# Attention on Trainium2: one Exp over four PSUM banks in place of two over two banks each

## The reference, cut to what matters

```
# per sequence: x is (2048, 1024), 16 heads of 64
h    = layernorm(x)
q    = h @ Wq + bq
k    = (h @ Wk + bk) @ Wl + bl
v    = (h @ Wv + bv) @ Wl + bl
attn = softmax(q k^T / 8)                # per head, 2048 x 2048
x    = x + layernorm((attn v) @ Wo + bo)
h2   = layernorm(x)
ffn  = h2 @ base_W.T + base_b
     + (h2 @ shared_A.T) @ shared_B.T
     + sum over the top 2 of 6 experts: weight * (h2 @ A_e.T) @ B_e.T
out  = x + layernorm(ffn)
```

## Time and profile before

| | |
|---|---|
| time of the runs, median (lowest to highest) | 4710.9 us (4707.45 to 4715.0) |
| the profiled execution's own time | 4704.67 us |
| its span, first to last instruction, core 7 (slowest) | 4703.1 us |
| spans of the other cores | 4646.7 to 4702.5 us |
| PE busy | 2743.8 us (58%) |
| DVE busy | 1551.9 us (33%) |
| ACT busy | 1297.1 us (28%) |
| stage B0, from its first QK to the last output projection's end | about 483 to 1865 us |
| stage B1, likewise | about 2322 to 3677 us |
| Exp: instructions, mean | 1024, 1.20 us |

### The profile page before, as it was taken

How to read it: one execution, slowest core, us unless ns; L and a number is a source line. 1 busy time by engine, 2 the same in 40 slices (tenths; PEclk the granted TensorE clock), 3 DMA queues, 4 the chain that set the end, 5 groups by cost and what they waited for, 6 DMA issues and landing times.

```text
span 4703.1 us, 32867 instructions; the slowest of 8 cores (4646.7 to 4703.1 us)
## 1 busy us (share of the span) xinstructions
PE 2743.8 (58%) x9296; PEld 843.8 (18%) x9296; DVE 1551.9 (33%) x2164; ACT 1297.1 (28%) x1117; POOL 10.1 (0%) x16
## 2 busy tenths in 40 slices
PE   4777566666666665667766566656666233333333
PEld 1333111111111111233211111111111111111111
DVE  2444122123222222444222322222222355444455
ACT  0000443443443443000144344454344000000000
POOL 0000000000000000000000000000000000000000
PEclk9888555555555555888955655665655666666666
DMA  5000100000000001100100000000000421222221
GB/s 108 19 18 2 17 0 0 18 0 0 18 0 18 0 0 32 40 19 19 18 0 0 18 0 0 18 0 0 18 0 0 112 88 73 80 81 90 90 76 67
DMA packets 52838, 137.00 MB, mean 29 GB/s; under 512 B 7479, under 2 KB 7614, under 8 KB 52670
## 3 DMA queue, kind: packets, MB, share of 16 engines
q1 hardware_dynamic: 42206, 117.59, 6.8%
q0 software_dynamic: 10464, 17.32, 2.3%
HBM read 101.87 MB, written 50.33 MB: 32 GB/s over the span
## 4 chain that ended last, share of the span: by engine, by line
PE 47%; DVE 23%; ACT 13%; issue 7%; ACTq 5%; DMA 4%; DVEq 1%; SPq 0%; another core or an unknown queue 0%; POOL 0%; POOLq 0%
PE ps L323 12%; ACT pt_sb L438 12%; DVE xn_fm L477 9%; PE ps L457 6%; PE ps L421 6%; PE ps L460 5%; PE psT L421 5%; ACTq L165 4%; PE ps L517 3%; PE ps L862 3%; PE ps L483 3%; DVE xn_fm L475 2%; DMA xst<-z_scr 1%; DVE k_sb L590 1%; DVE k_sb L894 1%
## 5 line engine op out<-in xcount | busy, mean ns | idle before, releaser
L438 ACT ACTIVATE pt_sb<-ps,cst_sb 128x1024 bf16<-128x1024 f32 x512 | 616.6, 1204 | 1311.8 <-PE ps L425 1279.5
L475 DVE COPY xn_fm<-ps 1x1024 f32<-1x1024 f32 x64 | 78.0, 1219 | 1845.5 <-PE ps L460 1845.5
L438 ACT ACTIVATE pt_sb<-psT,cst_sb 128x1024 bf16<-128x1024 f32 x512 | 616.0, 1203 | 136.9 <-PE psT L425 136.6
L457 PE MATMUL ps<-pt_sb,vt_sb 128*65 128x512 bf16 x1024 | 625.3, 611 | 40.2 <-ACTq L165 40.2
L460 PE MATMUL ps<-pt_sb,vt_sb 128*65 128x512 bf16 x1024 | 621.7, 607 | 0.0
L421 PE MATMUL ps<-q_sb,k_sb 64*128 64x512 bf16 x512 | 288.8, 564 | 411.9 <-ACTq L165 371.5
L483 PE MATMUL ps<-xn_fm,ones_sb 1*64 1x512 f32 x128 | 123.8, 1069 | 519.6 <-DVEq L165 519.6
L477 DVE RECIPROCAL xn_fm<-xn_fm 1x1024 f32<-1x1024 f32 x64 | 418.6, 6541 | 5.1
L323 PE MATMUL ps<-xn_fm,arena 128*128 128x512 bf16 x1536 | 354.4, 394 | 26.8 <-DMA blrow_bf<-blrow 15.9
L421 PE MATMUL psT<-q_sb,k_sb 64*128 64x512 bf16 x512 | 301.2, 588 | 0.0
L425 PE MATMUL psT<-q_sb,k_sb 64*128 64x512 bf16 x512 | 301.2, 588 | 0.0
(11 more groups left out here) (136 smaller groups left out, 2268.6 us busy)
## 6 DMA issues: line engine op xcount, KB each, us to landing
xst<-x SPq DMA_DIRECT2D x32, 512.0 KB, 6.2
z_scr<-xst SPq DMA_DIRECT2D x64, 256.0 KB, 3.2
xst<-z_scr SPq DMA_DIRECT2D x64, 256.0 KB, 5.0
k_sb<-x SPq DMA_DIRECT2D x32, 512.0 KB, 7.9
x_scr<-q_sb SPq DMA_DIRECT2D x32, 512.0 KB, 2.6
k_sb<-x_scr SPq DMA_DIRECT2D x32, 512.0 KB, 5.2
out<-q_sb SPq DMA_DIRECT2D x32, 512.0 KB, 2.6
arena<-wq POOLq DMA_DIRECT2D x2, 2048.0 KB, 21.2
```

The costliest lines, as they stand in the source:

```text
L438: return sc.activation(ptflat[:, pp, :], stb[pk][:, 0:1024], AF.Exp, bias=cst[:, 1:2], scale=cst[:, 0:1])
L457: t.matmul(avA[0:65, :], vt_sb[:, tkc, j, 0:65], pt_sb[:, pp, 0, :], start=(tkc == 0), stop=(tkc == 15))
L475: v.tensor_copy(den_sb[0:1, :], av2[64:65, :])
```

## The change

The two score buffers `ps1` and `psT` become one PSUM tensor `psB` of 2048 float32 columns (four banks); even chunks write its lower and odd chunks its upper 1024 columns, so every matmul writes where it wrote. One ACTIVATE now takes all 2048 columns of a pair, after the odd chunk's QK. The results of even pairs go to `pt_sb`, which shrinks from three chunk slots to two, the slots of one pair; those of odd pairs go to the upper two thirds of `xn_tok`, which grows from 2 to 3 rows of 1024. The QK of a pair wait for the Exp of the pair before. Stages A and C get other names for the same places, and no instruction there changes.

```
-        psT = ctx.enter_context(nc.psum_tensor("psT", [128, 2048], BF16))
+        psB = ctx.enter_context(nc.psum_tensor("psB", [128, 2048], F32))
+        ps1 = psB
+        psTb = psB.bitcast(BF16).reshape([128, 4096])
...
-            stb = [ps1[:, 0:1024], psTf[:, 0:1024]]
+            stb = [psB[:, 0:1024], psB[:, 1024:2048]]
...
+            ptw = [pt_sb.reshape([128, 2048])[:], xnt_flat[:, 1024:3072]]
...
                         pk = tkc % 2
-                        pp = tkc % 3
-                        wk_ = (j, tkc - 2) if tkc >= 2 else \
-                            ((j - 1, 14 + tkc) if j > 0 else (7, 14 + tkc))
+                        P = tkc // 2
+                        wk_ = (j, P - 1) if P >= 1 else \
+                            ((j - 1, 7) if j > 0 else (7, 7))
                         we = exp_done.get(wk_)
...
                         qk_done = inc("T", sT)
-                        wav = av_done.get((j, tkc - 3)) if tkc >= 3 else \
-                            av_done.get((j - 1, 13 + tkc) if j > 0 else (7, 13 + tkc))
-                        def fexp(sc, tkc=tkc, pk=pk, pp=pp, qk=qk_done, wav=wav):
-                            sc.wait_ge(sT.h, qk)
-                            if wav is not None:
-                                sc.wait_ge(sT.h, wav)
-                            return sc.activation(ptflat[:, pp, :], stb[pk][:, 0:1024],
-                                                 AF.Exp, bias=cst[:, 1:2],
-                                                 scale=cst[:, 0:1])
-                        Q["S"].append(fexp)
-                        if tkc % 2 == 1 or tkc == 15:
-                            exp_done[(j, tkc)] = inc("S", sS)
-                            exp_done[(j, tkc - 1)] = exp_done[(j, tkc)]
+                        if tkc % 2 == 1:
+                            wav_t = 2 * P - 3
+                            wav = av_done.get((j, wav_t)) if wav_t >= 0 else \
+                                av_done.get((j - 1, 16 + wav_t) if j > 0
+                                            else (7, 16 + wav_t))
+                            def fexp(sc, P=P, qk=qk_done, wav=wav):
+                                sc.wait_ge(sT.h, qk)
+                                if wav is not None:
+                                    sc.wait_ge(sT.h, wav)
+                                return sc.activation(ptw[P % 2],
+                                                     psB[:, 0:2048],
+                                                     AF.Exp, bias=cst[:, 1:2],
+                                                     scale=cst[:, 0:1])
+                            Q["S"].append(fexp)
+                            exp_done[(j, P)] = inc("S", sS)
...
                         def fav(t, j=j, tkc=tkc, pp=pp, ed=ed,
...
-                                     pt_sb[:, pp, 0, :],
+                                     pslot(tkc, 0),
```

More of the change, by code:

```diff
@@ L95, in build_nc @@
         stn = sb("stn", [128, NTT], F32)
-        xn_tok = sb("xn_tok", [128, 2, D], BF16)
+        xn_tok = sb("xn_tok", [128, 3, D], BF16)
         xn_fm = sb("xn_fm", [128, NCH, SLT], BF16)
@@ L101, in build_nc @@
         vt_sb = sb("vt_sb", [128, 16, 8, 130], BF16)
-        pt_sb = sb("pt_sb", [128, 3, 2, SLT], BF16)
-        pth = pt_sb.bitcast(F32).reshape([128, 1536])
+        pt_sb = sb("pt_sb", [128, 2, 2, SLT], BF16)
+        pth = pt_sb.bitcast(F32).reshape([128, 1024])
         dummy = pth[:, 0:1024]
@@ L134, in build_nc @@
         rden = fmh[0:1, 1024:2048]
-        xth = xn_tok.bitcast(F32).reshape([128, 1024])
+        xth = xn_tok.bitcast(F32).reshape([128, 1536])
+        xnt_flat = xn_tok.reshape([128, 3072])
         dr_sb = xth[:, 0:512]
@@ L138, in build_nc @@
         xn3_tok = ur[:, 2048:4096].rearrange("p (t d) -> p t d", t=2)
-        hs_brhs = pt_sb.reshape([128, 3072])[:, 0:SLT]
+        hs_brhs = pt_sb.reshape([128, 2048])[:, 0:SLT]
         lg_sb = xth[0:6, 0:512]
         w_fm = xth[0:6, 512:1024]
-        ps1 = ctx.enter_context(nc.psum_tensor("ps1", [128, 1024], F32))
-        psT = ctx.enter_context(nc.psum_tensor("psT", [128, 2048], BF16))
+        psB = ctx.enter_context(nc.psum_tensor("psB", [128, 2048], F32))
+        ps1 = psB
+        psTb = psB.bitcast(BF16).reshape([128, 4096])
         ps2 = ctx.enter_context(nc.psum_tensor("ps2", [128, 2048], F32))
@@ L291, in emit_phase_A @@
                     bank = "p%d" % (tt % 2)
-                    tp = psT[:, (tt % 2) * 1024:(tt % 2 + 1) * 1024]
+                    tp = psTb[:, 2048 + (tt % 2) * 1024:2048 + (tt % 2 + 1) * 1024]
                     Q["T"].append(lambda t, v=va: t.wait_ge(sV.h, v))
@@ L391, in emit_phase_B, with pslot @@
         def emit_phase_B(seq):
-            psTf = psT.bitcast(F32).reshape([128, 1024])
-            stb = [ps1[:, 0:1024], psTf[:, 0:1024]]
+            stb = [psB[:, 0:1024], psB[:, 1024:2048]]
             av2 = ps2[:, 0:1024]
             drb = [ps2[:, 1024:1536], ps2[:, 1536:2048]]
-            ptflat = pt_sb.reshape([128, 3, 1024])
+            ptw = [pt_sb.reshape([128, 2048])[:], xnt_flat[:, 1024:3072]]
+            def pslot(tkc, h):
+                s = tkc % 4
+                if s < 2:
+                    return pt_sb[:, s, h, :]
+                o = 1024 + (s - 2) * 1024 + h * SLT
+                return xnt_flat[:, o:o + SLT]
             exp_done = {}
@@ L408, in emit_qk @@
                         pk = tkc % 2
-                        pp = tkc % 3
-                        wk_ = (j, tkc - 2) if tkc >= 2 else \
-                            ((j - 1, 14 + tkc) if j > 0 else (7, 14 + tkc))
+                        P = tkc // 2
+                        wk_ = (j, P - 1) if P >= 1 else \
+                            ((j - 1, 7) if j > 0 else (7, 7))
                         we = exp_done.get(wk_)
-                        if we is None and wk_ in exp_done:
-                            we = exp_done.get((wk_[0], wk_[1] + 1))
                         def fqk(t, j=j, tkc=tkc, qb=qb, pk=pk, we=we,
@@ L431, in emit_qk @@
                         qk_done = inc("T", sT)
-                        wav = av_done.get((j, tkc - 3)) if tkc >= 3 else \
-                            av_done.get((j - 1, 13 + tkc) if j > 0 else (7, 13 + tkc))
-                        def fexp(sc, tkc=tkc, pk=pk, pp=pp, qk=qk_done, wav=wav):
-                            sc.wait_ge(sT.h, qk)
-                            if wav is not None:
-                                sc.wait_ge(sT.h, wav)
-                            return sc.activation(ptflat[:, pp, :], stb[pk][:, 0:1024],
-                                                 AF.Exp, bias=cst[:, 1:2],
-                                                 scale=cst[:, 0:1])
-                        Q["S"].append(fexp)
-                        if tkc % 2 == 1 or tkc == 15:
-                            exp_done[(j, tkc)] = inc("S", sS)
-                            exp_done[(j, tkc - 1)] = exp_done[(j, tkc)]
-                        else:
-                            exp_done[(j, tkc)] = None
+                        if tkc % 2 == 1:
[13 more added lines that the diff above has]
+                            exp_done[(j, P)] = inc("S", sS)
                     def emit_av(tkc):
-                        pp = tkc % 3
-                        ed = exp_done[(j, tkc)] or exp_done.get((j, tkc + 1))
+                        pp = tkc % 4
+                        ed = exp_done[(j, tkc // 2)]
                         wat = attn_done.get(j - 1 if j >= 1 else 7)
@@ L457, in fav @@
                             t.matmul(avA[0:65, :], vt_sb[:, tkc, j, 0:65],
-                                     pt_sb[:, pp, 0, :],
+                                     pslot(tkc, 0),
                                      start=(tkc == 0), stop=(tkc == 15))
                             return t.matmul(avB[0:65, :], vt_sb[:, tkc, j, 65:130],
-                                            pt_sb[:, pp, 1, :],
+                                            pslot(tkc, 1),
                                             start=(tkc == 0), stop=(tkc == 15))
@@ L546, in emit_phase_C @@
             ztp_keys = [("zA",), ("zB",)]
-            tp_bf = [psT[:, 0:1024], psT[:, 1024:2048]]
+            tp_bf = [psTb[:, 2048:3072], psTb[:, 3072:4096]]
             ha_ps = ps2[:, 0:512]
```

## The result

The changed kernel takes 5039.0 us (median of 10 runs, 5024.3 to 5096.6) against 4714.4 us (median of 10 runs) of the kernel before: ratio 1.0707, 95% interval 1.0672 to 1.0742. I had forecast slower, 5120 us, with a range of 5065 to 5205.

A forecast was written before the change was run, and what follows sets the result against it. Bound: a loop of waits between ACT and PE. 64 head steps at +6.19 us gave +396 on 4704.67, 5101; losing two thirds of 27 us of full-clock gain made 5119, forecast 5120 us, range 5065 to 5205.

The forecast's parts named there:

- The bound: Attention stages: a loop of waits between ACT and PE, paid once per pair, 3.68 us; no engine full.
- The price of 2048 columns: The merged Exp on ACT: 2.06 us taken, between bounds of 1.20 and 2.31 us.
- The line through 24 and 1024 columns: Other estimate of the merged Exp: 0.98 ns a column, so 2.21 us in all.
- Pairs and head step: Pairs 1 to 7: 4.54 us for 3.68; pair 0: 3.40 for 3.23; head step +6.19 us.
- The clock: PE's clock in attention: expected to rise more rarely, two thirds of a 27 us full-clock gain lost.
- these 27 us: What full-clock stretches in B1 gave the kernel before on core 7: 11 us plus 16 us.
- 396: Attention stages: us added by longer pairs, +6.19 us in each of 64 head steps.
- rival C: PE at full clock nearly throughout, raised by the longer pair: 4680 us, 0.6% faster; chance 0.02.
- case B: PE's clock stays as it is, full-clock head steps as often as before: 5095 us; chance 0.20.
- A: Long Exp saves nothing, 2.31 us: 5230 to 5257 us; chance 0.16, with the 2.21 case.
- D: ACT was the bound, only its work counts, 512 fixed costs saved: 4577 us; chance 0.01.

## Why the prediction was right, and where it was wrong

*The bound.* Right: the loop of ACT and PE, not ACT's work. Splitting the Exp again cost what the chain says, and a delay of the same length in the kernel before cost the same.

*The price of 2048 columns.* Right: 2.060 us measured, 2.06 taken, from the slope of the two small forms. The line through 24 and 1024 columns (2.21) was too high, so the Exp form does carry a larger fixed part: from 1024 to 2048 columns it grows by 0.84 ns a column, which leaves 0.35 us, against some 0.20 in the small rows. The estimate worked out from the Trainium skill ("ScalarE: Activation LUTs", section "What ACT_TABLE_LOAD costs") was 2.08 us, and the trace agrees within 1%.

*Pairs and head step.* Right: 4.53 us a pair against 4.54, 47.02 a head step against 47.0. Idle before an Exp in pairs 1 to 7 was 2.47 us (2.5 forecast), before the even QK 1.39 (1.40).

*The clock.* Wrong, and this is what put the time outside the range. The step was "I expect the clock to rise more rarely, and most of these 27 us to go". In its place the clock rose in four of five head steps. Over the 56 head steps of a core that the count covers, it gave back 56 x 2.13 = 119 us where before it gave 56 x 0.7 = 40. The rest of the sum closes with that: 396 - 79 = 317 us, and stages B0 and B1 together did grow by 319 us on the average of the cores (2720 to 3039), the other stages by 7. I had argued from PE's share of a pair, which did fall; the runs show that this share is not the whole of it. It fits the second half of what happened, that the clock fell again after some three pairs, but not the first, that it rose so often. A head step 0.27 us longer doubled the share that stays at half clock, so the exact times matter; why a pair of 4.53 us brings the clock up more often than one of 3.68 stays open. I should have given rival C's mechanism, a longer pair that changes the clock, a middle form and more than 0.02: three full-clock pairs in a head step, not seven. My case B, 5095 us, assumed that the clock could do no better than before, and that set the lower end of the range; nothing in the trace excluded a better one.

*The rule on idle time* (the Trainium skill, "TensorE: Matmul & The Clock Gate", section "A second HAM failure mode: psum-queue depth-cycling"), that short idle stretches between groups of matmuls make the clock swing between its two levels. The traces agree: in the changed kernel it rose and fell again inside 312 of 448 head steps, and with the gap filled it did so in none. What I had drawn from it, that more idle time per pair leaves less full clock, did not hold from before to changed: idle before the even QK at half clock went from 0.54 to 1.39 us, and there was more full clock in all.

*The rivals.* A fell with the 2.06 us. D fell too: every Exp waits for a QK. What a second pair of score buffers would do was not tried. B and C both had the clock doing at least as well as before; the truth lay between them, with 2.4 full-clock pairs in a head step where before there were 0.8.

## What to carry to other kernels

An instruction that is hidden costs nothing, and to merge it into the one behind it that is not hidden puts its work on the chain: work out what waits for what before counting instructions. The order of a pair's matmuls, which nobody had touched, was worth 5 to 6%, and in that order the merged Exp cost 29 us and not 325. Where PE sits at half clock in a loop with a short gap, a spare matmul in the gap is a cheap thing to try; here it gave 5.0% in the kernel before. Give a forecast over such a loop a wider range on both sides, since a quarter of a microsecond in a head step moved its clock.

## What the runs showed of the hardware that was not expected

- An ACTIVATE reads 2048 float32 columns from four PSUM banks at the same rate as from two: 0.84 ns for each column beyond 1024, and 0.86 from 732 to 1024 (0.954, 1.204 and 2.060 us for 732, 1024 and 2048). Two of 1024 back to back take 2.30 us.
- Once PE's clock had come up in the changed kernel it mostly stayed up for three pairs, on all cores: 260 of 448 head steps within 44.3 to 44.5 us, and 266 of 448 in another kernel with the same timing. The pair in which it came up varied: in the 260 it was pair 2 in 128, pair 3 in 78, pair 4 in 43 and pair 5 in 11.
- Matmuls whose results nobody reads made a kernel faster: by 220 us (two a pair) and 56 us (one a pair) in the changed kernel, by 5.0% in the kernel before.
